# Softplus as one ScalarE function, both halves together, in a scan and feed-forward kernel with its tile loop written out

## The chip, the core and the metric

The kernel runs on one core of one Trainium2 chip. The metric is the device time of one execution in microseconds (us). Time before: 1263.95 us, the median of 3 runs (1263.41 to 1265.72). The engines are PE (TensorE), DVE (VectorE), ACT (ScalarE), POOL (GpSimd) and SP, which here issues nearly all DMAs. PEld is the weight load of PE.

## The reference, cut to what matters

Four sequences of 1024 tokens with 256 channels pass a selective scan block with its own MLP, and then a gated feed-forward stage with a Walsh-Hadamard transform, each with a residual. The part that the change touches is dt:

```python
z, x, Bc, Cc, dt_raw = split(u @ in_proj_w.T)
dt = softplus(dt_raw @ dt_proj_w.T + dt_proj_b)      # 256 channels
dA = exp(dt * A)                                     # 32 states per channel
h  = dA * h + (dt * x) * B                           # scan along the sequence
y  = sum(h * C) + x * D
```

## The kernel before, in words

The tokens are cut into 8 tiles of 512; two tiles are one sequence. The 256 channels are two halves (h = 0, 1) of 128 partitions. A tile has U = 64 units u, each one scan of [128, 512]: PE spreads dt over the states (`spread`, L413), ACT makes exp(dt A) in place in PSUM (`decay`, L551), DVE scans (L791), POOL multiplies two units' states with C (L988), and PE sums them (L424). Ahead of the scan, dt * x is multiplied with B (`drive`), three of eight pairs on POOL (L968), the others on DVE (L776). Three PSUM banks hold spread dt, so spread of unit u + 3 waits for the scan of unit u.

Beside the units of tile i, each engine's `body` does the projections of tile i + 1 (`pre`: uT, dtr, xb, dtp0, dtp1, c0) and the MLP and feed-forward stages of tile i - 1 (`post`: out, hT, gate, up, down, xT, w1, w3, w2). All engines walk through the same 64 steps in program order and meet at semaphores. On PE these dense matmuls are put into steps by a planner: PLAN (L59) lists the stages with their cost, `place_steps` deals them out at the smallest rate that fits, STEPS holds what each step gets and ENDS the step in which a stage ends. The other engines' code asks for `ENDS[...] + n`. The dense results go through a ring of three PSUM banks (BANK: place in PLAN modulo 3), and before a stage writes its bank `bank_free` waits for the reader of the stage three places before it. Stages that end in steps 24 to 36 are: dtp0 24, down 28 and 31, c0 35, xT 36; dtp1 is in step 52, w2 in 56 and 61.

The softplus of a half is taken as max(v, 0) + log(1 + exp(-|v|)) with a correction. At s0 = ENDS of dtp: ACT takes Abs and Relu (s0 + 1, L583 and L584), Exp (s0 + 2, L587), Copy with +1 (s0 + 3, L592), Ln (s0 + 4, L597); DVE makes two corrections (s0 + 6 L854, s0 + 7 L859); POOL subtracts to get dt (s0 + 7, L999) and multiplies it with x (s0 + 8, L1003). Then dt is split into a high and a low part, by an ACT Copy (s0 + 9, L604) and a DVE subtraction (s0 + 11, at most 63, L868). SP stores dt * x as rows in DRAM (`keep_rows`, L291), from which `load_run` (L285) reads them four units at a time, and loads the split dt for PE (`load_dt`, L302). Half 0 does this around step 30, half 1 in steps 53 to 63. One set of buffers serves both halves.

`bodies` (L225) writes out bodies -1, 0 and 1, runs bodies 2 to 5 in a hardware loop of two rounds with register waits, and writes out bodies 6, 7 and 8. Body -1 has `pre` alone, bodies 7 and 8 have no `pre`.

## Time and profile before

| | us |
|---|---|
| median of 3 runs | 1263.95 |
| the profiled execution | 1264.71 |
| its span, first to last instruction | 1263.0 |
| PE busy | 1080.1 (86%) |
| DVE busy | 1065.1 (84%) |
| POOL busy | 958.0 (76%) |
| ACT busy | 636.1 (50%) |
| mean granted PE clock, of 2.4 GHz | 0.936 |

Busy time is the sum over one engine's instructions in the span. A timeline row gives start, duration, engine, line, operation, output and inputs, a count, and in brackets the idle time before it and who ended it. Consecutive instructions of one engine overlap by up to 0.1 us, and one row can hold several like instructions (x2). In a table of stretches PEclk is the granted clock, 1.00 for 2.4 GHz and 0.50 for 1.2 GHz.

### The profile page before, as it was taken

The numbers are of one execution on the slowest core, as the hardware profiler recorded it, in microseconds if no ns is written. First come the engines' busy times: TensorE is split into PE (matmuls) and PEld (weight loads), VectorE is DVE, ScalarE is ACT, GpSimd is POOL, SyncE is SP. The second block draws the span as 40 slices with busy tenths as digits, with TensorE's granted clock in tenths as the row PEclk, the third lists the DMA queues.
The fourth block names the chain that finished last, engine by engine and source line by source line (L and its number), as shares of the span: only waits on it lengthen the run. The fifth ranks groups of instructions, "written<-read, shape, count | busy, mean of one in ns | idle before, by whom it ended". The sixth has DMA issues, their size and how long they took to land.

```text
span 1263.0 us, 14738 instructions
## 1 busy us (share of the span) xinstructions
PE 1080.1 (86%) x3848; PEld 542.2 (43%) x3848; DVE 1065.1 (84%) x1193; ACT 636.1 (50%) x1142; POOL 958.0 (76%) x580
## 2 busy tenths in 40 slices
PE   2475649999798979899898989899898979898888
PEld 1121214535344444445444444445443544446445
DVE  3288999999998989999899889998999889996222
ACT  3755365545655465545655555545654545442210
POOL 0389998887998788887998888887998789865100
PEclk9676679999998999999899989999999999898889
DMA  5797867574866666684767675684766666650000
GB/s 195 170 250 162 200 152 164 121 179 105 196 134 155 146 156 144 133 187 112 173 136 164 141 165 130 135 187 110 188 135 142 147 154 133 134 117 17 1 0 17
DMA packets 99511, 176.55 MB, mean 140 GB/s; under 512 B 12960, under 2 KB 21600, under 8 KB 98784
## 3 DMA queue, kind: packets, MB, share of 16 engines
q1 hardware_dynamic: 98272, 171.36, 59.7%
q0 software_dynamic: 1152, 4.19, 0.9%
q8 instruction: 34, 0.56, 0.2%
q14 instruction: 53, 0.43, 0.1%
HBM read 150.34 MB, written 8.39 MB: 126 GB/s over the span
## 4 chain that ended last, share of the span: by engine, by line
POOL 29%; issue 25%; PE 16%; ACT 2%; DVE 2%; POOLq 1%; DVEq 0%; ACTq 0%
POOL h_s L988 16%; POOL bt_s L968 7%; PE p_r L458 5%; PE p_r L469 5%; PE p_r L464 2%; PE p_dt L413 2%; PE p_y L424 2%; POOL carry L985 1%; PE p_r L475 1%; POOL sp_l L999 1%; DVE h_s L791 1%; POOL res L1017 1%; POOL sp_w L1003 1%; POOL rs L957 1%; ACT p_dt L551 1%
## 5 line engine op out<-in xcount | busy, mean ns | idle before, releaser
L988 POOL TENSOR_TENSOR h_s<-h_s,c_s 128x1024 f32<-128x1024 f32 x256 | 607.9, 2376 | 104.5 <-DVE h_s L791 94.5
L551 ACT ACTIVATE p_dt<-p_dt,an_s 128x512 f32<-128x512 f32 x512 | 334.5, 658 | 308.1 <-PE p_dt L413 307.7
L413 PE MATMUL p_dt<-kdt,pick_s 128*128 128x512 f32 x512 | 349.5, 692 | 77.9 <-DVE h_s L791 75.5
L791 DVE TENSOR_TENSOR_SCAN h_s<-p_dt,carry,bt_s 128x512 f32<-128x512 f32 x256 | 320.6, 1270 | 14.1 <-ACT p_dt L551 13.6
L791 DVE TENSOR_TENSOR_SCAN h_s<-p_dt,bt_s 128x512 f32<-128x512 f32 x256 | 304.1, 1210 | 31.8 <-ACT p_dt L551 25.4
L469 PE MATMUL p_r<-nT,w_s 128*128 128x512 f32 x512 | 243.8, 604 | 5.4 <-ACT nT L716 5.4
L968 POOL TENSOR_TENSOR bt_s<-bt_s,b_s 128x1024 f32<-128x1024 f32 x96 | 227.2, 2367 | 19.1 <-DMA bt_s<-dx_rows 18.4
L413 PEld LDWEIGHTS p_dt<-kdt,pick_s 128*128 128x128 f32 x512 | 101.3, 201 | 222.9 <-DVE h_s L791 139.4
L776 DVE TENSOR_TENSOR bt_s<-bt_s,p_b 128x1024 f32<-128x1024 f32 x160 | 192.9, 1205 | 2.2 <-DMA bt_s<-dx_rows 1.0
L458 PE MATMUL p_r<-nT,gu_s 128*128 128x512 f32 x352 | 169.9, 603 | 2.3 <-ACT nT L711 2.3
L424 PE MATMUL p_y<-h_s,ysel_s 128*32 128x512 f32 x1024 | 150.5, 663 | 21.5 <-POOL h_s L988 21.5
L469 PEld LDWEIGHTS p_r<-nT,w_s 128*128 128x128 f32 x512 | 95.0, 191 | 122.4 <-issue 114.0
L475 PE MATMUL p_r<-w_s,hd_s 128*128 128x256 f32 x512 | 125.0, 385 | 0.0
L444 PE MATMUL p_r<-uT_s,in_s 128*128 128x512 f32 x192 | 107.2, 666 | 12.5 <-ACT uT_s L653 5.6
L475 PEld LDWEIGHTS p_r<-w_s,hd_s 128*128 128x128 f32 x512 | 96.7, 191 | 28.8 <-issue 14.9
L464 PE MATMUL p_r<-down_s,hd_s 128*128 128x256 f32 (+1 forms) x384 | 100.8, 394 | 0.0
L458 PEld LDWEIGHTS p_r<-nT,gu_s 128*128 128x128 f32 x352 | 64.8, 191 | 79.4 <-issue 73.6
L738 ACT ACTIVATE th_s<-p_r 128x512 f32<-128x512 f32 x64 | 38.2, 597 | 119.7 <-PE p_r L469 119.7
L464 PEld LDWEIGHTS p_r<-down_s,hd_s 128*128 128x128 f32 (+1 forms) x384 | 68.1, 188 | 35.2 <-issue 25.9
L930 DVE SCALAR_TENSOR_TENSOR th_s<-th_s,p_r 128x512 f32<-128x512 f32 x64 | 43.1, 674 | 35.6 <-ACT th_s L738 35.3
L439 PE MATMUL p_r<-ident_s,tok 128*128 128x128 f32 x192 | 31.8, 312 | 44.9 <-ACT tok L568 33.0
L985 POOL TENSOR_TENSOR carry<-h_s,one_s 128x2 f32<-128x2 f32 x128 | 30.1, 236 | 47.2 <-DVE h_s L791 46.3
(92 smaller groups left out, 857.3 us busy)
## 6 DMA issues: line engine op xcount, KB each, us to landing
bt_s<-dx_rows SPq DMA_DIRECT2D x512, 256.0 KB, 5.4
kdt<-st_dt SPq DMA_DIRECT2D x64, 128.0 KB, 3.8
tok<-in_x SPq DMA_DIRECT2D x8, 512.0 KB, 6.9
xr_s<-xb_s SPq DMA_DIRECT2D x64, 64.0 KB, 4.0
dx_rows<-sp_w SPq DMA_DIRECT2D x16, 256.0 KB, 2.0
b_s<-xb_s SPq DMA_DIRECT2D x64, 64.0 KB, 2.0
xo<-in_x SPq DMA_DIRECT2D x8, 512.0 KB, 7.1
out<-res POOLq DMA_DIRECT2D x8, 512.0 KB, 6.3
```

The costliest lines, as they stand in the source:

```text
L413: nc.tensor.matmul(p_dt[DT_BANK[u]][:, :], sel, kdt[:, h, p // 16, :], start=True, stop=True)\
L424: last = nc.tensor.matmul(p_y[32 * j:32 * j + 32, :], ysel_s[:, 28 - 4 * row:60 - 4 * row], h_s[:, u % 8, :], start=(m % 8 == 0), stop=(m ...
L444: ins = nc.tensor.matmul(ps[:, :], in_s[:, j, blk, :], uT_s[:, u_par, j, :], start=(j == 0), stop=(j == 1))
L458: ins = nc.tensor.matmul(ps[:, :], gu_s[:, j, blk, :], nT[:, j, :], start=(j == 0), stop=(j == 1))
L464: ins = nc.tensor.matmul(ps[:, D * (j // 6):D * (j // 6) + D], hd_s[0:n_in, f, P * s:P * s + P], down_s[0:n_in, f, :], start=(f == 0), sto ...
L469: ins = nc.tensor.matmul(ps[:, :], (w1_s if stage == "w1" else w3_s)[:, j, P * k:P * k + P], nT[:, j, :], start=(j == 0), stop=(j == 1))
L475: ins = nc.tensor.matmul(ps[:, D * (j // 8):D * (j // 8) + D], hd_s[:, f, P * s:P * s + P], w2_s[:, f, :], start=(f == 0), stop=(f == HB - 1))
L551: A(p_dt[DT_BANK[u]][:, :], p_dt[DT_BANK[u]][:, :], ACT.Exp, scale=an_s[:, c:c + 1]).then_inc(a_dA, 1)
L776: V.tensor_tensor(bt_s[:, two, :], bt_s[:, two, :], p_b[:, :].unsqueeze(1).broadcast_to([P, 2, T]), ALU.mult).then_inc(v_bt, 1)
L791: V.tensor_tensor_scan(h_s[:, u % 8, :], p_dt[DT_BANK[u]][:, :], bt_s[:, u % 16, :], carry[:, u:u + 1] if par else 0.0, ALU.mult, ALU.add) ...
L968: G.tensor_tensor(bt_s[:, two, :], bt_s[:, two, :], b_s[:, h, :].unsqueeze(1).broadcast_to([P, 2, T]), ALU.mult).then_inc(g_bt, 1)
L988: G.tensor_tensor(h_s[:, two, :], h_s[:, two, :], c_s[:, h, :].unsqueeze(1).broadcast_to([P, 2, T]), ALU.mult)\
```

## The change

Softplus becomes one ACT function, with the bias added in it, and both halves are taken one after the other in step 25, behind dtp1, which is moved next to dtp0 in PLAN. Each half has a buffer for dt (`dt_s`) and for its split (`st_dt`) of its own; dt * x has one (`dx_s`). The corrections on DVE and the subtraction on POOL fall away. The splits' Copy is at ENDS + 2 and + 3 on ACT, the low parts at + 4 and + 6 on DVE, dt * x at + 4 and + 12 on POOL, the rows are stored in steps 30 and 42 on SP. The order in PLAN changes the ring's banks. The loop over the middle bodies is written out.

```diff
-        + [("dtp0", 0, 1, .86)]
+        + [("dtp0", 0, 1, .86), ("dtp1", 0, 1, .86)]
...
-        + [("dtp1", 0, 1, .86)]
...
-DT_STEP = 12
+DT_STEP = 8
...
-            with eng.Fori(1, LAST // 2) as pair:
+            for pair in range(1, LAST // 2):
...
-                sp.dma_start(dx_rows[par, h], sp_w[:, :]).then_inc(l_rows, 16)
+                sp.dma_start(dx_rows[par, h], dx_s[:, :]).then_inc(l_rows, 16)
...
-                        if u == ENDS["dtp0", 0] + 10:
+                        if u == ENDS["dtp1", 0] + 6:
                             keep_rows(nt, 1 - par, 0)
-                        if u == max(32, ENDS["dtp0", 0] + DT_STEP):
+                        if u == max(32, ENDS["dtp1", 0] + DT_STEP):
                             load_dt(nt, 0)
                         if u == 34:
                             load_b(nt, 0)
+                        if u == 42:
+                            keep_rows(nt, 1 - par, 1)
...
                         if u == 63:
-                            keep_rows(nt, 1 - par, 1)
...
+            def softplus(t, u):
+
+                s0 = ENDS["dtp1", 0]
                 if u == s0 + 1:
...
+                    for h in range(2):
+                        m = t * 2 + h
+                        act.wait_ge(mm["dtp"], m + 1)
+                        if from_tile(t, 1):
+                            act.wait_ge(g_dx, m - 1)
+                            act.wait_ge(v_dtl, m - 1)
+                        A(dt_s[:, h, :], ring[BANK[f"dtp{h}", 0]][:, :], ACT.Softplus, bias=par_s[:, 4 + h:5 + h])\
+                            .then_inc(a_sp, 1)
+                for h in range(2):
+                    if u == s0 + 2 + h:
+                        act.wait_ge(a_sp, t * 2 + h + 1)
+                        if from_tile(t, 1):
+                            act.wait_ge(l_k[h], t * 64)
+                        A(st_dt[:, h, 0, :], dt_s[:, h, :], ACT.Copy).then_inc(a_dth, 1)
...
-                            if u == s0 + 6:
-
-                                dve.wait_ge(a_l, m + 1)
-                                V.scalar_tensor_tensor(out=sp_l[:, :], in0=sp_w[:, :], scalar=-1.0, in1=sp_l[:, :],
-                                                       op0=ALU.add, op1=ALU.subtract).then_inc(v_ln, 1)
-                            if u == s0 + 7:
-
-                                dve.wait_ge(v_ln, m + 1)
-                                V.scalar_tensor_tensor(out=sp_w[:, :], in0=sp_l[:, :], scalar=0.0, in1=sp_e[:, :],
-                                                       op0=ALU.max, op1=ALU.subtract).then_inc(v_c, 1)
-                            if u == min(s0 + 11, U - 1):
...
+                            s0, m = ENDS["dtp1", 0], nt * 2 + h
+                            if u == s0 + 4 + 2 * h:
...
                                 dve.wait_ge(a_dth, m + 1)
+                                V.tensor_tensor(st_dt[:, h, 1, :], dt_s[:, h, :], st_dt[:, h, 0, :].bitcast(F32),
+                                                ALU.subtract).then_inc(v_dtl, 1)
...
-                                G.tensor_tensor(sp_l[:, :], sp_r[:, :], sp_w[:, :], ALU.subtract).then_inc(g_dt, 1)
-                            if u == s0 + 8:
-                                pool.wait_ge(g_dt, m + 1)
+                            if u == s0 + 4 + 8 * h:
+                                pool.wait_ge(a_sp, m + 1)
                                 pool.wait_ge(l_xrep, (nt + 1) * 128)
+                                if h or from_tile(nt, 1):
+                                    pool.wait_ge(l_rows, m * 16)
+                                G.tensor_tensor(dx_s[:, :], dt_s[:, h, :], xr_s[:, other, h, :], ALU.mult)\
                                     .then_inc(g_dx, 1)
```

## Rows read from the trace of the kernel before

**Rows 1.** The page's head and part 1: busy us, share, instructions

```profile
span 1263.0 us, 14738 instructions
...
PE 1080.1 (86%) x3848; PEld 542.2 (43%) x3848; DVE 1065.1 (84%) x1193; ACT 636.1 (50%) x1142; POOL 958.0 (76%) x580
```

**Rows 2.** Table of stretches: start:end, length, busy us (count) per engine, clock, DMA

```profile
61.00:184.00 123.00, 75.36 (x218) 25.60 (x219) 109.15 (x104) 62.73 (x105) 114.36 (x81) 0.68 0.86 191
...
464.00:605.00 141.00, 129.60 (x479) 65.27 (x477) 133.86 (x149) 77.66 (x141) 118.05 (x60) 0.98 0.65 150
...
542.00:596.00 54.00, 53.79 (x196) 28.36 (x196) 50.75 (x61) 27.60 (x48) 39.70 (x18) 1.00 0.63 144
```

**Rows 3.** Timeline of DVE: first scans of tiles 0, 1 and 7

```profile
60.96 2.34 DVE L791 TENSOR_TENSOR_SCAN h_s<-p_dt,bt_s 128x512 f32<-128x512 f32 x2 [0.20 <-ACT p_dt L551]
...
183.88 2.44 DVE L791 TENSOR_TENSOR_SCAN h_s<-p_dt,carry,bt_s 128x512 f32<-128x512 f32 x2
...
1026.59 2.44 DVE L791 TENSOR_TENSOR_SCAN h_s<-p_dt,carry,bt_s 128x512 f32<-128x512 f32 x2
```

**Rows 4.** Groups by line: shapes, count, busy us, mean ns, idle us before

```profile
L868 DVE TENSOR_TENSOR st_dt<-sp_l,st_dt 128x512 fp32r<-128x512 f32 x16 | 23.9, 1497 | 10.1 <-ACT st_dt L604 10.1
...
L854 DVE SCALAR_TENSOR_TENSOR sp_l<-sp_w,sp_l 128x512 f32<-128x512 f32 x16 | 21.6, 1347 | 11.1 <-ACT sp_l L597 11.1
...
L597 ACT ACT_TABLE_LOAD x16 | 20.5, 1283 | 0.3
...
L999 POOL TENSOR_TENSOR sp_l<-sp_r,sp_w 128x512 f32<-128x512 f32 x16 | 20.3, 1266 | 17.4 <-DVE sp_w L859 17.4
...
L859 DVE SCALAR_TENSOR_TENSOR sp_w<-sp_l,sp_e 128x512 f32<-128x512 f32 x16 | 11.0, 688 | 0.0
L583 ACT ACTIVATE sp_e<-p_r,par_s 128x512 f32<-128x512 f32 x16 | 11.0, 686 | 2.3 <-PE p_r L448 2.2
```

**Rows 5.** Timelines of DVE and ACT, tile 3, u = 25 to 29

```profile
516.22 0.69 DVE L924 TENSOR_TENSOR hd_s<-th_s,p_r 64x512 f32<-64x512 f32 x1
...
518.08 2.45 DVE L791 TENSOR_TENSOR_SCAN h_s<-p_dt,carry,bt_s 128x512 f32<-128x512 f32 x2
...
519.95 0.66 ACT L551 ACTIVATE p_dt<-p_dt,an_s 128x512 f32<-128x512 f32 x1 [1.62 <-PE p_dt L413]
520.62 1.28 ACT L597 ACT_TABLE_LOAD   x1
521.92 0.63 ACT L597 ACTIVATE sp_l<-sp_w 128x512 f32<-128x512 f32 x1
522.57 1.28 ACT L551 ACT_TABLE_LOAD   x1
```

**Rows 6.** Timeline of PE, tile 3: first down matmuls, first w1 matmuls

```profile
514.89 1.89 PE L464 MATMUL p_r<-down_s,hd_s 128*128 128x256 f32 x8
...
542.03 1.95 PE L469 MATMUL p_r<-nT,w_s 128*128 128x512 f32 x4 [0.83 <-ACT nT L716]
```

**Rows 7.** Timelines of DVE and PE, tile 3, u = 56 to the next tile

```profile
584.28 2.46 DVE L791 TENSOR_TENSOR_SCAN h_s<-p_dt,carry,bt_s 128x512 f32<-128x512 f32 x2 [1.61 <-ACT p_dt L551]
...
589.35 1.28 DVE L791 TENSOR_TENSOR_SCAN h_s<-p_dt,carry,bt_s 128x512 f32<-128x512 f32 x1 [0.84 <-ACT p_dt L551]
...
598.95 0.50 PE L413 MATMUL p_dt<-kdt,pick_s 128*128 128x512 f32 x1 [2.61 <-DVE h_s L791]
...
604.32 1.22 DVE L776 TENSOR_TENSOR bt_s<-bt_s,p_b 128x1024 f32<-128x1024 f32 x1 [0.98 <-issue]
```

**Rows 8.** Timeline of POOL: first drive of tile 0

```profile
54.18 2.34 POOL L968 TENSOR_TENSOR bt_s<-bt_s,b_s 128x1024 f32<-128x1024 f32 x1 [14.93 <-DMA bt_s<-dx_rows]
```

**Rows 9.** Timelines of PE and DVE, last stage: first down matmul, gate 5's product

```profile
1195.03 5.33 PE L464 MATMUL p_r<-down_s,hd_s 128*128 128x256 f32 x22
...
1196.57 0.69 DVE L924 TENSOR_TENSOR hd_s<-th_s,p_r 64x512 f32<-64x512 f32 x1
```

More of the change, by code:

```diff
@@ L156, in build @@
         xb_s = sb("xb_s", [P, T])
[L157 to L162 removed]
+        dt_s = sb("dt_s", [P, 2, T])
+        dx_s = sb("dx_s", [P, T])
+        st_dt = sb("st_dt", [P, 2, 2, T], F32R)
         res = sb("res", [P, 2, SUB, D])
@@ L201, in build @@
         a_b = [sem(f"a_b{h}") for h in range(2)]
-        a_abs, a_rel, a_e, a_w, a_l, a_dth, a_zt = (sem(f"a_{n}") for n in
-                                                   ("abs", "rel", "e", "w", "l", "dth", "zt"))
+        a_sp, a_dt, a_dth, a_zt = (sem(f"a_{n}") for n in ("sp", "dt", "dth", "zt"))
         a_sq, a_hn, a_hT, a_gt, a_xn, a_xT, a_ft = (sem(f"a_{n}") for n in
@@ L206, in build @@
         a_ve, a_kept, a_ms, a_ve2 = (sem(f"a_{n}") for n in ("ve", "kept", "ms", "ve2"))
-        v_bt, v_sc, v_st, v_mv, v_zs, v_ln, v_c, v_dtl = (
-            sem(f"v_{n}") for n in ("bt", "sc", "st", "mv", "zs", "ln", "c", "dtl"))
+        v_bt, v_sc, v_st, v_mv, v_zs, v_dtl = (sem(f"v_{n}") for n in ("bt", "sc", "st", "mv", "zs", "dtl"))
         v_yf, v_yz, v_h, v_ga, v_mh, v_x1, v_st2, v_mv2 = (
@@ L214, in build @@
         g_rr, g_rr2, g_car, g_bt = sem("g_rr"), sem("g_rr2"), sem("g_car"), sem("g_bt")
-        g_hc, g_r, g_r2, g_r3, g_dt, g_dx, g_hx = (sem(f"g_{n}") for n in
-                                                            ("hc", "r", "r2", "r3", "dt", "dx", "hx"))
+        g_hc, g_r, g_r2, g_r3, g_dx, g_hx = (sem(f"g_{n}") for n in ("hc", "r", "r2", "r3", "dx", "hx"))
         dx_rows = nc.dram_tensor("dx_rows", [2, 2, P, T], F32).ap()
@@ L367, in _ @@
         def _(pe):
-            freed = {"uT": (a_uT, 2), "dtr": (a_dtr, 1), "xb": (a_xb, 1), "dtp0": (a_rel, 2), "dtp1": (a_rel, 2),
+            freed = {"uT": (a_uT, 2), "dtr": (a_dtr, 1), "xb": (a_xb, 1), "dtp0": (a_sp, 2), "dtp1": (a_sp, 2),
                      "z": (v_zs, 2), "c0": (a_c[0], 1), "c1": (a_c[1], 1), "out": (v_h, 2), "hT": (a_hT, 2),
@@ L493, in body @@
                 for u in range(U):
-                    if known(i) and i == -1 and u == ENDS["dtp1", 0] + 1:
+                    if known(i) and i == -1 and u == ENDS["c0", 0] + 1:
                         transform_w2()
@@ L570, in normalise @@
                 ins.then_inc(signal, 1)
-            def softplus(t, u, h):
-                s0 = ENDS[f"dtp{h}", 0]
-                m = t * 2 + h
+            def softplus(t, u):
+                s0 = ENDS["dtp1", 0]
                 if u == s0 + 1:
-                    act.wait_ge(mm["dtp"], m + 1)
-                    if h or from_tile(t, 1):
-                        act.wait_ge(v_c, m)
-                        act.wait_ge(g_dt, m)
-                    v = ring[BANK[f"dtp{h}", 0]][:, :]
-                    A(sp_e[:, :], v, ACT.Abs, bias=par_s[:, 4 + h:5 + h]).then_inc(a_abs, 1)
-                    A(sp_r[:, :], v, ACT.Relu, bias=par_s[:, 4 + h:5 + h]).then_inc(a_rel, 1)
-                if u == s0 + 2:
-                    act.wait_ge(a_abs, m + 1)
-                    A(sp_e[:, :], sp_e[:, :], ACT.Exp, scale=-1.0).then_inc(a_e, 1)
-                if u == s0 + 3:
-                    act.wait_ge(a_e, m + 1)
-                    if h or from_tile(t, 1):
-                        act.wait_ge(l_rows, m * 16)
-                    A(sp_w[:, :], sp_e[:, :], ACT.Copy, bias=1.0).then_inc(a_w, 1)
-                if u == s0 + 4:
-                    act.wait_ge(a_w, m + 1)
-                    if h or from_tile(t, 1):
-                        act.wait_ge(v_dtl, m)
-                    A(sp_l[:, :], sp_w[:, :], ACT.Ln).then_inc(a_l, 1)
-                if u == s0 + 9:
-                    if h:
-                        act.wait_ge(l_k[0], (t + 1) * 64)
-                    elif from_tile(t, 1):
-                        act.wait_ge(l_k[1], t * 64)
-                    act.wait_ge(g_dt, m + 1)
-                    A(st_dt[:, 0, :], sp_l[:, :], ACT.Copy).then_inc(a_dth, 1)
@@ L610, in body @@
                         scale_weights()
-                    if known(i) and i == -1 and u == ENDS["dtp1", 0] + 5:
+                    if known(i) and i == -1 and u == ENDS["c0", 0] + 5:
                         keep_w2()
@@ L670, in body @@
                             A(xb_s[:, :], ring[BANK["xb", 0]][:, :], ACT.Copy).then_inc(a_xb, 1)
-                        for h in range(2):
-                            softplus(nt, u, h)
+                        softplus(nt, u)
                     if units and u == XL_SLOT:
```

24 lines of the change are left out of this document (5 added, 19 removed).

## The prediction

> **What bounds the kernel now.** I read the busy shares first [rows 1]: PE and DVE are both near 85% of the span, so the average alone names no bound. The table of stretches comes next [rows 2]. In tile 0 (61 to 184 us) POOL is busy 114.4 of 123 us and PE only 75.4: that tile runs at POOL's pace. In a steady tile (464 to 605) DVE is busy 133.9 of 141, PE 129.6 and POOL 118.1: DVE is nearly full and PE close behind. The first scans of tiles give the periods [rows 3]: tile 0 takes 183.88 - 60.96 = 122.9 us, tiles 1 to 6 take (1026.59 - 183.88) / 6 = 140.5 us each. Then the timelines of one steady tile (tile 3), at its two softplus places. At the end of the tile (u = 53 to 63) DVE waits 1.61 and 0.84 us for decays of ACT, which is busy with softplus, and PE then waits 2.61 us for DVE [rows 7]. Between the two places, from the first w1 matmul on, PE leaves no gap: 53.8 of the 54 us from 542 to 596 [rows 2]. So the pace is DVE's around softplus and PE's in the dense stages, and what DVE sheds counts only up to PE's own waits.
>
> **What DVE, POOL and ACT shed.** Two of DVE's three operations per half go: L854 (1.35 us) and L859 (0.69) [rows 4], 2.03 per half and 4.07 per tile. The high-low split L868 (1.50) stays, but that of half 1 moves from u = 63 to u = 30. POOL sheds L999, 1.27 per half, 2.53 per tile [rows 4]. ACT sheds Abs, Relu, Exp, Copy and Ln and gets one Softplus; the trace has none, so I bound it by the ACT operations it has, 0.63 (Ln [rows 5]) and 0.69 (Abs with a bias vector, out of PSUM [rows 4]), and take 0.69, since operands and shape are those of Abs.
>
> **Table loads.** Before, each Ln takes a load (16 [rows 4]) and the Exp after it another [rows 5], so four per steady tile of 1.28 us. The groups have loads at Ln and behind it, and none between Exp, Tanh, Copy, Abs and Relu. Which set Softplus is in no row shows. The bounds are no load at all and, with both halves in a row, two per tile; I take two, as Ln is its nearest neighbour. The Trainium skill ("ScalarE: Activation LUTs", table sets) says that a set has one expensive anchor and that the cheap functions are in all of them, and does not name Softplus; that points the same way.
>
> **The middle of the tile.** ACT's block is now, with no decay inside, 1.28 + 2 x 0.69 + 1.28, 3.9 us, where before it was 1.28 + 0.63 + 1.28 = 3.2 [rows 5] with the other operations strewn between decays. On the timeline of [rows 5] half 0 would be ready at 514.9, so the block ends at 518.8 to 519.3 and decay 27 behind it at 519.9. DVE started scan 27 at 519.3, the second of the pair at 518.08. Behind the waiting ACT stand decays 27 and 28 and the two splits' copies, and DVE's scans behind the decays: 0.6 us of new idle DVE per tile. Its bounds are nothing (no loads) and the block's whole 3.9. DVE there loses 2.03 of work and gains the second L868 (1.50) and 0.6 of waiting: in sum nothing.
>
> **A rule against this.** The trace has a load at 520.62, as the decay before it ends (519.95 + 0.66), and Ln at 521.92 [rows 5]: a switch costs 1.30 here. The Trainium skill ("ScalarE: Activation LUTs", what ACT_TABLE_LOAD costs) adds a drain of some 1380 ns, 2.66 us per switch. By that, as an estimate, the block would be 6.7 us and DVE's idle 3.4 instead of 0.6. The row has no such drain, and I go by the row; what a longer block would do is rival (e).
>
> **PE in the middle.** The plan is arithmetic: with dtp1 behind dtp0 the rate falls from 1.68 to 1.67, dtp1 is in step 24, down 0 still ends in 28, down 1 in 32 (was 31), xT and all w steps come one later. The ring turns: down 0 now has the bank of gate 5, not of up 4. PE must wait for gate 5's product (L924, 516.22 + 0.69 = 516.9 [rows 5]) before its first down matmul, which began at 514.89 [rows 6]. Half of this hides behind dtp1, moved there (0.86, two passes of 0.43 by the planner's own cost, which the dense pace of [rows 6], 1.95 for four, agrees with); PE idles about 1.0 us, and spread 28 behind it is late but still ahead of its scan. The first w1 matmul was at 542.03 [rows 6]; with step 37 in place of 36 I put it 1.0 us later.
>
> **The end of the tile.** PE then has the same list less dtp1's 0.86. It was dense until 596 and waited there 2.61 for DVE [rows 7]; now it comes to that point at 596.0 + 1.0 - 0.9 = 596.1. DVE is not behind PE there, as it lost 2.03 + 1.50 of work and, with ACT free, the waits of 1.61 and 0.84. PE needs its rest, some 3 us of w2, spreads and a y sum: 599. Then comes the result's addition, and then DVE's drive, which started at 604.32 with 0.98 of idle at the loop's end in it [rows 7], so at 603.3 without; now at 599.9. That is -3.4 us per tile, for six tiles -20.4. Bounds: PE regains only its 2.61 less the 1.0 and 0.6 above, -1.0; DVE gets it all, -4.07 - 2.45 + 0.6, -5.9.
>
> **Ahead of that.** POOL's chain from the first drive (54.18, after 14.93 of waiting for rows [rows 8]) has L999 and L1003 of half 1 in it, 2.53, now done earlier. Against it the first row load may be issued 1 us later: SP now has the row store of half 1 in front of it, which waits for POOL's product, and this for the landing of half 0's rows. In sum -1.5. Tile 0 runs at POOL's pace: -2.53. Together -4.0, between -5 and 0.
>
> **Loop written out.** DVE idles 0.98 at the loop's end [rows 7], once: -1.0. Cheaper waits in straight code could make it -3, code fetched once only 0.
>
> **What gets dearer.** Tile 7 and the last stage have no softplus but the same ring, and down 0 waits for gate 5. In the last stage PE began down at 1195.03, and that product is ready at 1196.57 + 0.69 = 1197.26 [rows 9]: +2.2. In tile 7 +1.0. On SP the row store of half 1 moves from u = 63 to 42 and half 0's from 34 to 30, past the loads of b_s and kdt; POOL's half 1 product at u = 36 waits for half 0's store, made some steps of 2.2 us earlier (140.5 / 64). Steps cover this, so nothing; in the prologue, which has no steps of that length, it is the 1 us above.
>
> **Sum.** -20.4 - 4.0 - 1.0 + 2.2 + 1.0 = -22.2 us. The profiled run's span is 1263.0 [rows 1], its time 1264.7, which is 0.8 above the median 1263.95. So 1242.5 against it and, as a median, 1242.
>
> **Rivals.**
> (a) The forecast, 1242: 0.52.
> (b) PE is the bound: its list is not shortened, and its waits come back elsewhere. Gain 1.2 per tile: -7.2 - 1.8 = -9, 1255. For it speaks the dense w stage, against it the wait of 2.61. 0.20.
> (c) DVE gets all, or Softplus shares Exp's table and nothing is loaded: 5.2 per tile, -31.2 - 1.8, 1231. For it speaks DVE's 133.9 us, against it PE's list. 0.13.
> (d) Slower: ACT's block stands in the stage where DVE and PE have no slack. From a DVE idle of 4.3 per tile on, instead of 0.6, the whole gain is gone. If all of the block shows (3.9), PE's bank wait in full (2.1 us) and PE is granted 1.2 GHz for a while after it (tile 0, where PE idles much, has a mean of 0.68 [rows 2]), 1.7 more, a tile pays 7.7 for the 6.0 of the upper bound: +10.2 - 1.8, 1272. 0.08.
> (e) It does not do what it says: tables are loaded around each Softplus, or a load costs twice. The block is 6.5, DVE's idle 3.2 and the gain per tile 0.8: -4.8 - 1.8, 1257. 0.04.
> (f) Gain and cost come out even: 0.03.
>
> **Range and chances.** 1231 (c) to 1257 (b, e). A measurement of this kernel can tell about 0.2%, 2.5 us. Faster: 0.52 + 0.20 + 0.13 + half of (e) = 0.87. Same: (f) and the other half, 0.05. Slower: 0.08.
>
> **What would show it.** Two table loads per tile, close together in ACT's timeline; a DVE gap of about 0.6 us at u = 27, ended by ACT; no DVE wait for ACT from u = 56 on; PE's wait of 2.61 us gone or under 1; the first down matmul about 2 us after its old place; periods of 137 us in tiles 1 to 6 and 120.4 in tile 0; the last stage 2 us longer. Wrong would be: DVE gaps above 2 us behind the block, L868 much above 1.50 now that both stand in the middle, or PE gaps that only move.

## The result and the profile after

The changed kernel takes 1258.62 us (median of 6 runs, 1253.71 to 1261.26) against 1264.03 for the kernel before (6 runs, 1263.41 to 1265.72). The ratio is 0.9948, with a 95% interval of 0.9935 to 0.9962. That is 5.4 us faster, where 22 were forecast. The time lies 1.6 us above the forecast's range of 1231 to 1257.

| | before | after |
|---|---|---|
| median, us | 1264.03 | 1258.62 |
| the profiled execution | 1264.71 | 1261.26 |
| its span | 1263.0 | 1259.5 |
| mean granted PE clock, of 2.4 GHz | 0.936 | 0.920 |

The profiled execution of after is the slowest of its six, 2.6 us above their median. Stretches are therefore compared within it, and its span is 3.5 us shorter than that of before, not 5.4.

Head and part 1 of the page of after (busy us, share of the span, instructions), which answer to [rows 1]:

```profile
span 1259.5 us, 12980 instructions
...
PE 1092.7 (87%) x3848; PEld 548.3 (44%) x3848; DVE 1033.5 (82%) x1161; ACT 579.6 (46%) x1062; POOL 929.1 (74%) x564
```

The work went as the diff says: DVE sheds 31.6 us, ACT 56.5, POOL 28.9. PE has the same 3848 matmuls and is busy 12.6 us longer. That is the first sign: the mean granted clock went from 0.936 to 0.920.

Timeline of DVE in after, the first scans of tiles 0, 1, 2, 3, 4 and 7, and the last scan of tile 7:

```profile
54.35 2.34 DVE L770 TENSOR_TENSOR_SCAN h_s<-p_dt,bt_s 128x512 f32<-128x512 f32 x2 [1.27 <-POOL bt_s L935]
...
174.26 2.57 DVE L770 TENSOR_TENSOR_SCAN h_s<-p_dt,carry,bt_s 128x512 f32<-128x512 f32 x2 [0.17 <-PE p_y L419]
...
317.85 2.33 DVE L770 TENSOR_TENSOR_SCAN h_s<-p_dt,bt_s 128x512 f32<-128x512 f32 x2
...
457.49 2.45 DVE L770 TENSOR_TENSOR_SCAN h_s<-p_dt,carry,bt_s 128x512 f32<-128x512 f32 x2
...
597.73 2.33 DVE L770 TENSOR_TENSOR_SCAN h_s<-p_dt,bt_s 128x512 f32<-128x512 f32 x2
...
1017.28 2.45 DVE L770 TENSOR_TENSOR_SCAN h_s<-p_dt,carry,bt_s 128x512 f32<-128x512 f32 x2
...
1149.60 1.28 DVE L770 TENSOR_TENSOR_SCAN h_s<-p_dt,carry,bt_s 128x512 f32<-128x512 f32 x1 [0.68 <-ACT p_dt L546]
```

Three scans of before that [rows 3] doesn't have, the first of tiles 3 and 4 and the last of tile 7:

```profile
464.50 2.45 DVE L791 TENSOR_TENSOR_SCAN h_s<-p_dt,carry,bt_s 128x512 f32<-128x512 f32 x2
...
605.45 2.33 DVE L791 TENSOR_TENSOR_SCAN h_s<-p_dt,bt_s 128x512 f32<-128x512 f32 x2
...
1155.46 1.28 DVE L791 TENSOR_TENSOR_SCAN h_s<-p_dt,carry,bt_s 128x512 f32<-128x512 f32 x1 [0.25 <-ACT p_dt L551]
```

With [rows 3] these give the whole span, stretch by stretch:

| stretch | before | after | difference | forecast |
|---|---|---|---|---|
| up to the first scan | 60.96 | 54.35 | -6.6 | -1.5 |
| tile 0 | 122.9 | 119.9 | -3.0 | -2.5 |
| tiles 1 to 6 | 842.7 | 843.0 | +0.3 | -20.4, and -1.0 for the loop |
| tile 7 | 130.2 | 133.6 | +3.4 | +1.0 |
| behind the last scan | 106.3 | 108.6 | +2.3 | +2.2 |

So the six steady tiles, on which nearly all of the forecast stood, gained nothing. Tile 3, measured from its first scan on, shows where: the last w2 work and the tile's end became 5.0 us shorter, more than foreseen, and by then PE was 4.3 us late.

| tile 3, us after its first scan | before | after |
|---|---|---|
| first down matmul | 50.4 | 51.2 |
| first w1 matmul | 77.5 | 80.7 |
| first w2 matmul | 114.4 | 118.7 |
| first scan of tile 4 | 141.0 | 140.2 |

The first w2 matmuls of after and of before (the others stand in [rows 6] and below):

```profile
576.20 1.89 PE L470 MATMUL p_r<-w_s,hd_s 128*128 128x256 f32 x8
```

```profile
578.92 1.03 PE L475 MATMUL p_r<-w_s,hd_s 128*128 128x256 f32 x4
```

**Where the 3 to 4 us arise.** ACT of after, tile 3: a decay, the copy of the c0 product, then the token normalisation.

```profile
530.21 0.66 ACT L546 ACTIVATE p_dt<-p_dt,an_s 128x512 f32<-128x512 f32 x1 [2.30 <-PE p_dt L408]
533.63 0.60 ACT L638 ACTIVATE c_s<-p_r 128x512 f32<-128x512 f32 x1 [2.75 <-PE p_r L439]
534.12 2.06 ACT L563 ACTIVATE tok<-res,mb,rs 128x256 f32<-128x256 f32 x4
```

POOL of after: the statistics that this normalisation needs.

```profile
529.85 0.20 POOL L991 TENSOR_TENSOR mb<-nm,rs 128x4 f32<-128x4 f32 x1
```

PE of after at the same place: the spread before c0, c0 (L439), the transposes of xT (L434) and the first w1 matmul (L464).

```profile
529.38 0.79 PE L408 MATMUL p_dt<-kdt,pick_s 128*128 128x512 f32 x1 [2.65 <-DVE h_s L770]
529.98 3.62 PE L439 MATMUL p_r<-uT_s,in_s 128*128 128x512 f32 x4
...
536.33 1.94 PE L434 MATMUL p_r<-ident_s,tok 128*128 128x128 f32 x8 [1.88 <-ACT tok L563]
538.19 2.04 PE L464 MATMUL p_r<-nT,w_s 128*128 128x512 f32 x2
```

The normalisation could have begun at 530.9, since its statistics were ready at 530.05 and the decay at 530.21 had ended (0.66). It began at 534.12, because the copy of c_s stands ahead of it in ACT's order and waits for PE's c0. That c0 took 3.62 us for four matmul records (c0 is two fp32 matmuls of 512 columns, and the trace has two records for each). PE then waits 1.88 us for the normalised tokens. In the kernel before, the order of these two was the other way round. ACT:

```profile
537.70 2.08 ACT L568 ACTIVATE tok<-res,mb,rs 128x256 f32<-128x256 f32 x4 [1.69 <-POOL mb L1026]
...
540.25 0.58 ACT L658 ACTIVATE c_s<-p_r 128x512 f32<-128x512 f32 x1
```

PE of before, xT's transposes, without a wait:

```profile
540.17 1.04 PE L439 MATMUL p_r<-ident_s,tok 128*128 128x128 f32 x8
```

No line of the diff touches either instruction. The normalisation is bound to `ENDS["down", 1] + 4` and the copy to `ENDS["c0", 0] + 1`. With dtp1 moved, down 1 ends in step 32 and not in 31, while c0 stays in 35. Both now fall in step 36, and there the copy comes first in the code. The Trainium skill ("TensorE: Matmul & The Clock Gate", "Architectural detail: the array is 16× 32×32, not 1× 128×128") says that ACT is strictly first in, first out. The two rows of the copy and the normalisation in after agree: work that is ready waits 3.2 us behind a copy that is not.

Table of stretches, tile 3 from 528 to 542 us (busy us and count of PE, PEld, DVE, ACT, POOL; granted clock; DMA share; GB/s), of before:

```profile
528.00:542.00 14.00, 10.09 (x37) 4.99 (x36) 13.93 (x19) 7.77 (x16) 13.00 (x8) 0.88 0.54 129
```

and of after:

```profile
528.00:542.00 14.00, 10.73 (x20) 5.26 (x20) 9.68 (x10) 5.55 (x11) 12.52 (x8) 0.52 0.69 150
```

In after PE is granted 1.2 GHz through nearly all of this stretch (0.52), where before it had 0.88, and its 10.7 us of busy time hold 20 matmul records instead of 37. The window stands 7 us later in the tile of after than in that of before, so I also took the same part of every tile: from 60 to 95 us after the first scans of tiles 1 to 6, the half clock lasts 20 us in sum before (mean granted clock 0.95) and 72 us after (0.83). Both kernels have pauses of PE here. In after the pauses are followed by half clock that lasts into the first w1 matmuls.

### The profile page after: what moved, and what is told of

The parts are those of the page before. It is cut to its first block and busy times, and to the rows that moved or that the text cites. A ratio compares the mean times of both kernels' runs of the same rounds, so it can differ in the third digit from the quotient of the medians.

```text
span 1259.5 us, 12980 instructions
## 1 busy us (share of the span) xinstructions
PE 1092.7 (87%) x3848; PEld 548.3 (44%) x3848; DVE 1033.5 (82%) x1161; ACT 579.6 (46%) x1062; POOL 929.1 (74%) x564
## 5 line engine op out<-in xcount | busy, mean ns | idle before, releaser
L408 PE MATMUL p_dt<-kdt,pick_s 128*128 128x512 f32 x512 | 354.7, 706 | 57.6 <-DVE h_s L770 57.3
L464 PE MATMUL p_r<-nT,w_s 128*128 128x512 f32 x512 | 254.4, 626 | 1.7 <-ACT nT L695 1.7
L408 PEld LDWEIGHTS p_dt<-kdt,pick_s 128*128 128x128 f32 x512 | 104.4, 206 | 198.5 <-DVE h_s L770 113.8
L419 PE MATMUL p_y<-h_s,ysel_s 128*32 128x512 f32 x1024 | 146.3, 645 | 20.6 <-POOL h_s L955 20.6
L464 PEld LDWEIGHTS p_r<-nT,w_s 128*128 128x128 f32 x512 | 97.5, 196 | 122.0 <-issue 115.3
L439 PE MATMUL p_r<-uT_s,in_s 128*128 128x512 f32 x192 | 109.4, 686 | 9.5 <-ACT uT_s L633 5.0
L459 PE MATMUL p_r<-down_s,hd_s 128*128 128x256 f32 (+1 forms) x384 | 104.3, 401 | 7.3 <-DVE hd_s L891 7.3
L434 PE MATMUL p_r<-ident_s,tok 128*128 128x128 f32 x192 | 33.5, 324 | 51.9 <-ACT tok L563 40.6
L952 POOL TENSOR_TENSOR carry<-h_s,one_s 128x2 f32<-128x2 f32 x128 | 25.0, 195 | 55.3 <-DVE h_s L770 54.7
```

Of the source, the lines that this page charges most:

```text
L408: nc.tensor.matmul(p_dt[DT_BANK[u]][:, :], sel, kdt[:, h, p // 16, :], start=True, stop=True)\
L419: last = nc.tensor.matmul(p_y[32 * j:32 * j + 32, :], ysel_s[:, 28 - 4 * row:60 - 4 * row], h_s[:, u % 8, :], start=(m % 8 == 0), stop=(m ...
L439: ins = nc.tensor.matmul(ps[:, :], in_s[:, j, blk, :], uT_s[:, u_par, j, :], start=(j == 0), stop=(j == 1))
L459: ins = nc.tensor.matmul(ps[:, D * (j // 6):D * (j // 6) + D], hd_s[0:n_in, f, P * s:P * s + P], down_s[0:n_in, f, :], start=(f == 0), sto ...
L464: ins = nc.tensor.matmul(ps[:, :], (w1_s if stage == "w1" else w3_s)[:, j, P * k:P * k + P], nT[:, j, :], start=(j == 0), stop=(j == 1))
```

## The experiments

Each median stands beside the kernel before on the same chip, and the ratio with its 95% interval is against that. The letters A, B and C are those of each expectation. Periods are from a tile's first scan to the next one's, from the profiled runs.

**1. The loop alone.** The kernel before with its tile loop written out.

```diff
-            with eng.Fori(1, LAST // 2) as pair:
+            for pair in range(1, LAST // 2):
```

> The kernel before with its loop written out and nothing else. If writing out the loop is worth what I took for it (1.0 us, the 0.98 us of idle DVE at the loop's end), the time is 1262 to 1263.5. If register waits inside the loop cost as well, it is 1260 to 1261.5. If it costs nothing either way, 1264.

1261.91 us, ratio 0.9985 (0.9972 to 0.9999), 1.6 us below the 1263.52 of the kernel before on that chip. The forecast of 1.0 lies in the interval. 1261.9 is from now on the base for experiments that keep the plan or the softplus of before.

**2. xT a step earlier.** The changed kernel with the pace of the gate held and xT's transposes in step 36 instead of 37.

```diff
-         ("c0", 0): (("down", 1), 3), ("xT", 0): (("down", 1), GAP)}
+         ("c0", 0): (("down", 1), 3), ("xT", 0): (("down", 1), GAP - 1)}
...
-STEPS, ENDS = next(placed for placed in (place_steps(r / 100) for r in range(120, 300)) if placed)
+STEPS, ENDS = place_steps(1.67)
```

> The changed kernel with the gap ahead of xT one step shorter, so that xT and all w1, w3 and w2 steps go back to where they were before the change (xT in step 36, w2 ending in 61), all else the same. Theory A (the third empty PE step, 36, lets PE idle and its clock fall to 1.2 GHz for longer, as the w stage begins): the first w1 matmul comes 2 to 3 us earlier than the 80.6 us after the tile's start that the changed kernel has, half-clock stretches there shrink from 10 to 14 us per tile towards 3 to 7, and the time is 1240 to 1250. Theory B (the loss is the wait for gate 5's product and ACT's block, ahead of step 30): nothing moves by more than 1 us per tile, 1255 to 1260.

1267.73 us, ratio 1.0026 (1.0016 to 1.0037): 9 us worse than the changed kernel. In its trace the normalisation of tile 3 still stands behind the copy of c_s. PE, tile 3:

```profile
538.36 1.94 PE L434 MATMUL p_r<-ident_s,tok 128*128 128x128 f32 x8 [2.51 <-ACT tok L563]
```

c0, just ahead, runs at full clock here:

```profile
533.74 1.88 PE L439 MATMUL p_r<-uT_s,in_s 128*128 128x512 f32 x4
```

So theory A was right that the clock would recover (half clock of 3.4 us in this part of tile 3 instead of 13.7) and wrong about the time: PE waits 2.51 us instead of 1.88, and the first w1 matmul comes at 81.6 us, later than the 80.7 of the changed kernel. Theory B's 1255 to 1260 failed too. Tiles 1 to 6 take 140.7 us in the mean, as in the changed kernel (140.5). Of the 6.6 us between the two profiled spans they have about 1, and the rest lies ahead of the first scan, in tiles 0 and 7 and in the last stage. Less half clock alone brings nothing, then, while the normalised tokens come late.

**3. Fill in PE's pauses.** The changed kernel, with two fp32 matmuls of no use in each of steps 33, 34 and 36 of bodies 1 to 6, into banks that are free there.

```diff
+FILL = {33: ("c0", 2), 34: ("c0", 2), 36: ("xT", 2)}
...
+                    for _ in range(n):
+                        nc.tensor.matmul(ring[q % RING][:, :], in_s[:, 0, 2, :], uT_s[:, u_par, 0, :],
+                                         start=True, stop=True)
...
+                    if pre and post and u in FILL:
+                        fill(*FILL[u])
```

> The changed kernel with idle work for PE: two fp32 matmuls of 512 columns, whose result nobody reads, in each of the steps 33, 34 and 36 of bodies 1 to 6 (5 us of PE time per tile at full clock). Theory A (the clock is what is lost): PE stays at 2.4 GHz in the middle of tiles 1 to 6, the half-clock stretches there vanish or fall to 3.4 us, and the time drops to 1235 to 1248 although PE has 30 us more to do. Theory B (PE is short of time there, not of clock): the time rises by up to 5 us per tile, to 1260 to 1285.

1243.10 us, ratio 0.9828 (0.9812 to 0.9845). Work of no use makes the kernel 15.5 us faster. Its stretch in tile 3:

```profile
528.00:542.00 14.00, 12.87 (x47) 5.75 (x49) 11.47 (x13) 6.99 (x13) 11.33 (x6) 1.00 0.73 175
```

PE, c0 of tile 3:

```profile
524.42 1.88 PE L440 MATMUL p_r<-uT_s,in_s 128*128 128x512 f32 x4
```

The clock is 1.00 where it was 0.52 (this window stands 6 us later in the tile, but no part of this tile 3 is at half clock), c0's four records take 1.88 us instead of 3.62, and the first w1 matmul comes 78.8 us after the first scan instead of 80.7. The order on ACT is still the wrong one, but the copy now waits 1.05 us for c0 instead of 2.75. The Trainium skill ("TensorE: Matmul & The Clock Gate", "Loop structure matters more than you think") says that matmuls issued back to back keep PE's full clock and that a long wait between them loses it. These two traces agree in kind: 1.00 with the fill, 0.52 with pauses of 2.65 and 1.88 us.

**4. No table loads.** The changed kernel with Relu in the place of Softplus; dt is another function of the same input.

```diff
-                        A(dt_s[:, h, :], ring[BANK[f"dtp{h}", 0]][:, :], ACT.Softplus, bias=par_s[:, 4 + h:5 + h])\
+                        A(dt_s[:, h, :], ring[BANK[f"dtp{h}", 0]][:, :], ACT.Relu, bias=par_s[:, 4 + h:5 + h])\
```

> The changed kernel with Relu in place of Softplus, with the same operands and bias, so that dt is another function of its input: no table is loaded around it, and ACT's block in step 25 shrinks from 3.9 us to 1.3. If the block costs the 0.6 us per tile of idle DVE that I put in the sum, the time falls by 3 to 5 us, to 1254 to 1256. If the block is what took the expected gain, it falls by 12 to 20 us. If it is hidden, it falls by less than 2.

1249.01 us, ratio 0.9883 (0.9861 to 0.9905): 9.6 us below the changed kernel, more than the direct price and less than the whole loss, though only 0.3 us of DVE's time stands directly behind the block (below). Experiments 10 and 13 take this up.

**5. The function at its old places.** One Softplus per half, each half where the kernel before has it, so four table loads per tile, with the old plan and ring; loop written out.

```diff
+                for h in range(2):
+                    m = t * 2 + h
+                    if u == ENDS[f"dtp{h}", 0] + 1:
...
+                        A(dt_s[:, h, :], ring[BANK[f"dtp{h}", 0]][:, :], ACT.Softplus, bias=par_s[:, 4 + h:5 + h])\
+                            .then_inc(a_sp, 1)
```

> The changed kernel with Softplus as one function and the loop written out, but each half at its old place (dtp1 back in step 52, four table loads per tile, the old ring of banks and the old steps of xT, w1 and w2). If the loss lies in the place (the shifted plan, the late first w1 matmul, 80.6 us after the tile's start instead of 77.5), the first w1 matmul is back at 76 to 77.5 and the end of the tile still gains from what DVE sheds: 1235 to 1248. If DVE's shed work is worth nothing whatever the place, it is 1258 to 1262, that of the old kernel with its loop written out.

1244.89 us, ratio 0.9846 (0.983 to 0.9861). The function gives 17.0 us of 1261.9, and with it what follows it, since each half's split, its product with x and the row store also come some steps earlier than before. The order on ACT is as before here, with the normalisation ahead of the copy, and the clock in tile 3's stretch is 1.00. This is the run that separates function and place: the changed kernel is 13.7 us above it.

**6. Fill in the kernel before.** The kernel before, loop written out, with the fill of experiment 3 in the like steps (32, 33, 35).

```diff
+FILL = {32: ("c0", 2), 33: ("c0", 2), 35: ("xT", 2)}
```

> The kernel before with its loop written out, and the same idle work for PE that took the changed kernel to 1243.1: two fp32 matmuls in each of the three steps around the middle's gap (32, 33 and 35 here). If the idle work helps any kernel alike, this one falls by 12 to 16 us from 1261.9, to 1246 to 1250. If it only gives back a clock that the change had cost, this one, with half-clock stretches of 3.4 us in most tiles, falls by 2 to 8 us, to 1254 to 1260.

1259.53 us, ratio 0.996 (0.9947 to 0.9974): 2.4 us below 1261.9, against 15.5 in the changed kernel. The half clock of that part of tiles 1 to 6 goes to nothing in both, from 27 us in experiment 1 and from 72 in the changed kernel. So most of the loss is the changed kernel's own.

**7. Fill in tile 7 too.** Experiment 3 with body 7 included.

```diff
-                    if pre and post and u in FILL:
+                    if units and post and u in FILL:
```

> The kernel with PE's idle work in steps 33, 34 and 36, now in body 7 too. Tile 7 took 135.4 us without it, with 6.8, 3.4 and 10.2 us at half clock in and ahead of it, against 130.2 in the kernel before. If the clock is what tile 7 lacks, it falls to 131 to 133 and the time to 1239 to 1241. If it is the wait for gate 5's product and nothing else, it stays within 1 us of 1243.1.

1237.62 us, ratio 0.9791 (0.9773 to 0.9809), 5.5 below experiment 3 and a little more than I expected. Tile 7 takes 131.5 us instead of 135.4: what it lost beyond the forecast was clock too.

**8. The order on ACT mended.** The changed kernel, with only the copy of c_s one step later, so that the normalisation is ahead of it again.

```diff
-                        if u == ENDS["c0", 0] + 1:
+                        if u == ENDS["c0", 0] + 2:
```

> The changed kernel with ACT's copy of c0 one step later (37), so that the normalisation of the tokens for xT no longer stands behind it in ACT's queue. In the changed kernel ACT waits 2.75 us for c0 there, with the normalisation's inputs ready, and PE then waits 1.88 us for the result. If this queueing is what the middle loses, PE's wait of 1.88 us is under 0.6, the first w1 matmul comes 2 to 3 us earlier than 80.6 and the time is 1240 to 1248. If the clock has fallen already and PE's c0 is late whatever ACT does, the first w1 matmul moves by less than 1.5 us and the time is 1250 to 1258.

1242.36 us, ratio 0.9814 (0.9791 to 0.9836). One number in one line gives 16.3 us, and the time is what the forecast said of the whole change. ACT, tile 3:

```profile
524.44 2.06 ACT L563 ACTIVATE tok<-res,mb,rs 128x256 f32<-128x256 f32 x4
...
528.28 0.59 ACT L638 ACTIVATE c_s<-p_r 128x512 f32<-128x512 f32 x1
```

PE, tile 3:

```profile
523.02 0.80 PE L408 MATMUL p_dt<-kdt,pick_s 128*128 128x512 f32 x1 [2.64 <-DVE h_s L770]
523.62 3.62 PE L439 MATMUL p_r<-uT_s,in_s 128*128 128x512 f32 x4
...
527.89 1.67 PE L434 MATMUL p_r<-ident_s,tok 128*128 128x128 f32 x8
530.08 1.95 PE L464 MATMUL p_r<-nT,w_s 128*128 128x512 f32 x4 [0.52 <-ACT nT L695]
```

The pause of 2.64 us before c0 is still there, and so is c0 at half clock (3.62). But the transposes no longer wait, and after 0.52 us more the w1 matmuls run at full rate (four records in 1.95) instead of two in 2.04. They begin 78.9 us after the first scan, not 80.7. The half clock in that part of tiles 1 to 6 is 31 us instead of 72. Nothing but the copy's place differs between the two kernels, so the second wait, 1.88 us in the changed kernel, is what kept the clock down.

**9. Both mends.** Experiment 8 with the fill of experiment 7.

```diff
+FILL = {33: ("c0", 2), 34: ("c0", 2), 36: ("xT", 2)}
...
-                        if u == ENDS["c0", 0] + 1:
+                        if u == ENDS["c0", 0] + 2:
```

> The changed kernel with both mends: ScalarE's c_s copy one step later, and the two small matmuls of no use in each of three gaps of PE, in bodies 1 to 7. Theory A (the queue on ScalarE and the half clock are one loss: the late xT makes the gap, the gap makes the clock fall): the two gains don't add; whichever is applied second brings only what is left of the half clock, 1232 to 1238, next to 1237.6 of the fill alone and 1242.4 of the copy alone. Theory B (two losses of their own, 16 and 21 us): they add to 1222 to 1228. Theory C (fill in a gap that is gone costs its own time on PE): above 1242.

1232.58 us, ratio 0.9751 (0.9735 to 0.9766). Gains of 16.3 (copy) and 21.0 (fill) come to 26.0 together, so A: 11 of the copy's 16 us are in the fill's 21, and each has a part of its own. This version, with the whole computation, is the fastest of all: 2.5% below the kernel before.

**10. No table loads, order mended.** Experiment 8 with Relu in the place of Softplus.

```diff
-                        A(dt_s[:, h, :], ring[BANK[f"dtp{h}", 0]][:, :], ACT.Softplus, bias=par_s[:, 4 + h:5 + h])\
+                        A(dt_s[:, h, :], ring[BANK[f"dtp{h}", 0]][:, :], ACT.Relu, bias=par_s[:, 4 + h:5 + h])\
...
-                        if u == ENDS["c0", 0] + 1:
+                        if u == ENDS["c0", 0] + 2:
```

> The changed kernel with ScalarE's c_s copy one step later, and Relu in the place of Softplus, which changes dt to another function and leaves the table loads between the two functions out. It prices the loads once the queue is mended. Theory A (the block of loads costs little of itself, 0.3 to 0.6 us of DVE a tile, and the 9.6 us that it cost in the changed kernel went by way of the late xT): 1237 to 1241, 1 to 5 us below the 1242.4 with loads. Theory B (the block costs its 9.6 us whatever the queue): 1231 to 1234.

1233.18 us, ratio 0.9757 (0.9741 to 0.9774). My theory A fell: 9.2 us, as before the mend. DVE, the first pair of the w stage in tile 3, in experiment 8:

```profile
532.70 0.69 DVE L897 SCALAR_TENSOR_TENSOR th_s<-th_s,p_r 128x512 f32<-128x512 f32 x1 [1.47 <-ACT th_s L717]
```

and here:

```profile
529.31 0.69 DVE L897 SCALAR_TENSOR_TENSOR th_s<-th_s,p_r 128x512 f32<-128x512 f32 x1 [0.78 <-ACT th_s L717]
```

The wait differs over 20 us behind the block, at the place where PE is slow. That left two readings, which experiment 13 tells apart.

**11. xT a step earlier, order mended.** Experiments 2 and 8 together.

```diff
-         ("c0", 0): (("down", 1), 3), ("xT", 0): (("down", 1), GAP)}
+         ("c0", 0): (("down", 1), 3), ("xT", 0): (("down", 1), GAP - 1)}
...
-                        if u == ENDS["c0", 0] + 1:
+                        if u == ENDS["c0", 0] + 2:
```

> The changed kernel with ScalarE's c_s copy one step later, and xT's transposes one step earlier (step 36) with the gate's rate held at 1.67. Theory A (the earlier xT failed before only because the token normalisation came late behind the c_s copy): now at least even with the copy alone, 1238 to 1243. Theory B (an xT in step 36 moves the empty time of PE to the start of the next tile, whoever comes first on ScalarE): worse than the copy alone by the 9 us of before, 1249 to 1253.

1247.67 us, ratio 0.9859 (0.9841 to 0.9876): 5.3 above experiment 8. My theory A fell here as well, and B is nearer, though its 9 us were too many. An early xT costs of itself.

**12. The wrong order in the kernel before.** The kernel before, loop written out, with ACT's normalisation one step later, behind the copy. Softplus, plan and ring are untouched.

```diff
-                        if u == ENDS["down", 1] + 4:
+                        if u == ENDS["down", 1] + 5:
```

> The kernel before with its tile loop written out and one thing more: ScalarE's token normalisation ends one step later (step 36), so that it stands behind the c_s copy, as in the changed kernel; the softplus is as before. Theory A (the order of these two on ScalarE alone costs the time, in any kernel): xT later, the first w1 matmul 2 to 3 us later after the first scan, more of the span at 1.2 GHz, 1270 to 1285 against 1261.9 written out. Theory B (it costs only together with the moved down and gate of the changed kernel): 1260 to 1265.

1284.85 us, ratio 1.0159 (1.0145 to 1.0173): 22.9 us slower than 1261.9. ACT, tile 3:

```profile
549.22 0.66 ACT L551 ACTIVATE p_dt<-p_dt,an_s 128x512 f32<-128x512 f32 x1 [3.08 <-PE p_dt L413]
550.25 0.60 ACT L658 ACTIVATE c_s<-p_r 128x512 f32<-128x512 f32 x1 [0.37 <-PE p_r L444]
550.74 2.06 ACT L568 ACTIVATE tok<-res,mb,rs 128x256 f32<-128x256 f32 x4
```

PE, tile 3:

```profile
552.95 1.94 PE L439 MATMUL p_r<-ident_s,tok 128*128 128x128 f32 x8 [2.50 <-ACT tok L568]
```

The same signature: the normalisation behind the copy, then a wait of 2.50 us, then eight transposes in 1.94 us instead of 1.04. But this edit does more than swap two instructions. A step later the normalisation also stands behind one more decay, and that decay has most of the wait (3.08 us for PE's spread, the copy 0.37); the statistics were ready at 547.80, 2.9 us before the normalisation began. Tile 7, which has no copy, shows the decay's part by itself: 132.7 us instead of the 130.1 of experiment 1. So 22.9 us is the price of a normalisation that stands one step too late in ACT's order, with softplus, plan and ring as they were. The copy alone is what experiment 8 moves, and it is worth 16.3. Together they show the cause: the place of the normalisation in ACT's order, behind work that waits for PE.

**13. No table loads, with both mends.** Experiment 9 with Relu in the place of Softplus.

```diff
+FILL = {33: ("c0", 2), 34: ("c0", 2), 36: ("xT", 2)}
...
-                        A(dt_s[:, h, :], ring[BANK[f"dtp{h}", 0]][:, :], ACT.Softplus, bias=par_s[:, 4 + h:5 + h])\
+                        A(dt_s[:, h, :], ring[BANK[f"dtp{h}", 0]][:, :], ACT.Relu, bias=par_s[:, 4 + h:5 + h])\
...
-                        if u == ENDS["c0", 0] + 1:
+                        if u == ENDS["c0", 0] + 2:
```

> The kernel with both mends (copy one step later, fill in bodies 1 to 7), and Relu in the place of Softplus: dt is another function, and the table loads between the two functions are left out. Theory A (the loads cost mostly by way of TensorE's half clock, which the fill has taken away already; left is the first scan 1 us later and some 0.3 us of VectorE a tile): 1228 to 1231, that is 2 to 4 us below the 1232.6 with loads. Theory B (the loads cost their 9 us on the chain itself): 1222 to 1225.

1230.58 us, ratio 0.9731 (0.9718 to 0.9744): 2.0 us below experiment 9, as A had it. With PE's pauses filled, the loads cost 2.0 us in all. The other 7 of the 9 us of experiments 4 and 10 went by way of PE's pauses and the clock: in that part of tiles 1 to 6 the half clock lasts 31 us in experiment 8 and 17 in experiment 10.

**14. Fill with the halves at their old places.** Experiment 5 with two small matmuls in each of steps 32, 33 and 35, bodies 1 to 7.

```diff
+FILL = {32: ("c0", 2), 33: ("c0", 2), 35: ("xT", 2)}
...
+                    if units and post and u in FILL:
+                        fill(*FILL[u])
```

> The one function with each half at its old place (four loads a tile, the plan of before, loop written out), with two small matmuls of no use in each of three gaps of PE, in bodies 1 to 7. Without the fill it was 1244.9; the kernel before gained 2.4 us from such a fill. Theory A (the end of the stage is worth something by itself: 7 blocks of two loads fewer, no wait in gate 5): above the 1232.6 of the kernel with both mends, 1238 to 1243. Theory B (the place is worth nothing, the whole gain is the function): 1231 to 1235.

1247.12 us (1241.37 to 1251.05), ratio 0.9866 (0.9843 to 0.9888). Both theories missed: I had 1238 to 1243 and 1231 to 1235. The fill does raise the clock, from 0.935 to 0.954 over the profiled span, and tiles 1 to 6 take as long as without it (138.5 us in the mean, 138.2 in experiment 5). The copy of c_s now waits 1.67 us for c0, and tile 3's first w1 matmul comes at 77.6 us instead of 76.9. So the half clock that was left there was worth no more than what the fill itself costs. Both halves in a row at the end of the gate stage, with ACT's order mended, come out 2.5 us under the old places (1244.9 to 1242.4). That is not clear of noise, as the two intervals touch. With the fill it is 12 to 15 us (1244.9 or 1247.1 to 1232.6), and no run splits that up.

The 1261.9 to 1258.6 of the change, without the loop, is then -17.0 for the function and its followers (experiment 1 to 5), -2.5 for the place (5 to 8, not clear of noise), and +16.3 for the order on ACT (8 to the changed kernel). These are differences along one row of kernels, so they add up by construction.

## Why the prediction was wrong

**The step that failed** is "PE in the middle", its last sentence: with step 37 in place of 36 I put the first w1 matmul 1.0 us later. It came 3.2 us later after tile 3's first scan, the first w2 matmul 4.3, and so the term of -20.4 for tiles 1 to 6 measured +0.3. I had moved all steps that hang on down 1 by one, and then costed PE's own list. I did not list what else on ACT, DVE and POOL hangs on down 1, nor what stands next to it in the same step. The normalisation went from step 35 to 36, where c_s's copy was. Nothing in the trace of before shows this wait; the code and the planner's arithmetic do. Experiment 8 shows it as the cause: with the copy out of the way the first w1 matmul comes 1.4 us later than before, near the 1.0 that I had put, and the kernel is 16.3 us faster. Experiment 12 shows the same lateness in the kernel before, for 22.9 us.

**A second fault** lay in the price of pauses. I let PE's clock fall only in rival (d), by 1.7 us a tile. The trace showed this already, as PE had 0.88 from 528 to 542 before. The waits ahead of the w stage have to be priced with the half clock behind them, as experiments 3, 8 and 10 show. Experiments 2 and 14 set a limit to this: there the clock rose and the time did not fall.

**Removed work.** Right: the groups of after have two loads for two halves, 8 + 8 instead of 32, and Softplus costs 0.684 us where I took 0.69. L868's like, L835, costs 1.10 instead of 1.50. After, groups by line (shapes, count, busy us, mean ns, idle before):

```profile
L835 DVE TENSOR_TENSOR st_dt<-dt_s,st_dt 128x512 fp32r<-128x512 f32 x16 | 17.5, 1097 | 8.3 <-ACT st_dt L584 8.3
...
L577 ACT ACT_TABLE_LOAD x8 | 10.3, 1283 | 0.1
L546 ACT ACT_TABLE_LOAD x8 | 10.3, 1283 | 0.1
L577 ACT ACTIVATE dt_s<-p_r,par_s 128x512 f32<-128x512 f32 x16 | 10.1, 684 | 0.1
```

**The block on ACT.** 3.9 us as forecast, from 506.82 to 510.70, and no drain beyond the load: Softplus starts 1.30 us after its load did. ACT, tile 3:

```profile
506.82 1.28 ACT L577 ACT_TABLE_LOAD   x1
508.12 1.27 ACT L577 ACTIVATE dt_s<-p_r,par_s 128x512 f32<-128x512 f32 x2
509.40 1.28 ACT L546 ACT_TABLE_LOAD   x1
510.70 0.66 ACT L546 ACTIVATE p_dt<-p_dt,an_s 128x512 f32<-128x512 f32 x1
```

DVE behind it, the only wait that the block leaves there:

```profile
511.39 1.28 DVE L770 TENSOR_TENSOR_SCAN h_s<-p_dt,carry,bt_s 128x512 f32<-128x512 f32 x1 [0.26 <-ACT p_dt L546]
```

That is 0.26 instead of 0.6. Leaving the loads out saves 2.0 us in the run with both mends, 0.3 per tile, which is that wait, and 9 where the clock falls.

**PE's wait for gate 5.** Right: 0.92 for 1.0. The first down matmul came 0.9 us after its old place, where my list of signs had about 2.

```profile
508.74 1.56 PE L459 MATMUL p_r<-down_s,hd_s 128*128 128x256 f32 x6 [0.92 <-DVE hd_s L891]
```

**The end of the tile.** Right, and even better than forecast. PE's wait of 2.61 [rows 7] is gone, and now DVE waits for PE, as I had it:

```profile
595.99 0.69 DVE L872 TENSOR_TENSOR res<-p_r,res 128x512 f32<-128x512 f32 x1 [1.60 <-PE p_r L470]
```

From the first w2 matmul to the next first scan it is 21.5 us, before 26.5. But a gain at the end is only seen if PE comes there on time. The periods of tiles 1 to 6 in experiment 8 are 136.5 us in the mean, where I forecast 137.1, and 136.0 in experiment 9. Of the signs that the forecast would be wrong one came true: PE gaps that only move.

That experiment 8 lands on the forecast time is in part luck. Its tiles 1 to 6 bear out the term for the steady tiles, but tile 7 takes 135.0 us where I had 131.2, and an earlier first scan and shorter tiles 0 to 6 make up for it.

Two rivals were near in number, and neither for its reason. (b), 1255: PE's list was no bound; PE was late and slow. (e), 1257: there are two loads of 1.28 us per tile and no more. Of (d) one part came true, that PE is granted 1.2 GHz behind a pause, but the block on ACT was not what brought the pause.

**Ahead of that.** Mis-sized: -6.6 to the first scan instead of -1.5, and -3.0 in tile 0 instead of -2.5. POOL's first drive and the issue of the row load on SP, after:

```profile
51.90 2.35 POOL L935 TENSOR_TENSOR bt_s<-bt_s,b_s 128x1024 f32<-128x1024 f32 x1 [12.28 <-DMA bt_s<-dx_rows]
```

```profile
42.92 6.33 SPq L279 DMA_DIRECT2D bt_s<-dx_rows  x12
```

The same issue in before:

```profile
45.41 6.04 SPq L285 DMA_DIRECT2D bt_s<-dx_rows  x12
```

The drive began at 51.90 instead of 54.18 [rows 8], since the row load was issued 2.5 us earlier and not 1 us later. Behind it the scan came 2.4 us later and not 6.8, as POOL's subtraction of half 1, its split and the table load behind Ln no longer lay between. The first scan differs from run to run, though: 55.8 to 57.1 in experiments 8 to 11 and 13. So some 2 us of the 6.6 are this run's.

**The loop** gives 1.6 (forecast 1.0). **Tile 7** lost 3.4 instead of 1.0, and with both mends takes 131.1 us: +0.9, near the forecast, though with fill in it. **The last stage** is right, +2.3 for +2.2. PE, first down matmul of the last stage, and DVE's product ahead of it:

```profile
1189.70 10.66 PE L459 MATMUL p_r<-down_s,hd_s 128*128 128x256 f32 x36 [2.12 <-DVE hd_s L891]
```

```profile
1188.96 0.69 DVE L891 TENSOR_TENSOR hd_s<-th_s,p_r 64x512 f32<-64x512 f32 x1
```

**What stays open.** Why the earlier xT costs 5.3 us of itself (experiment 11) was not pursued. In the changed kernel, tile 1 took 143.6 us and its neighbours 140; in experiment 8 it still takes 139.2 against 136, so something of it is not ACT's order. In both runs POOL has tile 1's statistics ready 75.9 us after the first scan, and those of tiles 2 to 6 at 72.5 to 73.4; no run followed this up. And a 2.65 us pause of PE before c0 remains, which only the fill covers; no run filled it with useful work. Whether the changed ring and the earlier split and stores have prices of their own was not run apart from the rest.

## What to carry to other kernels

When one stage moves by a step, list every instruction on every engine that is bound to it, and look at the order in each step where they now land: ACT took its work in order, and one copy that waited ahead of a ready normalisation cost 16 us here, a normalisation one step too late 23. Price a pause of PE with the half clock that follows it. When a change touches the time little, undo its parts one by one: with the halves at their old places the function gave 17 us, and the move took nearly all of that back.
